# One block for both attentions, the top-1 stage and the experts, with the top-1 stage's first group computed inside the first attention

## The reference

```python
x = x + cross_attention(LN(x), ctx)     # 16 heads of 8, with biases
x = x + top1_ffn(LN(x))                 # 8 experts, one 128x128 matrix each
x = x + causal_attention(LN(x), ctx)    # keys and values again from ctx
x = x + top2_ffn(LN(x))                 # 8 experts, hidden width 352, SiLU gate

def top1_ffn(x):                        # x is LN(x) here
    chosen = argmax(x @ gate_w.T)       # 8 scores for each token
    return x + (x @ expert_w[chosen].T)
```

## Time and profile before

| what | value |
|---|---|
| median of 3 runs | 794.02 us (790.98 to 795.57) |
| the profiled execution | 793.19 us, its span 791.5 us |
| granted TensorE clock, mean | 0.907 of full speed |
| busy: PE, DVE, ACT, POOL | 78%, 61%, 50%, 45% |
| first attention, first to last instruction | 114.68 to 259.59 us of the span |
| first `choose` of the top-1 stage | 270.94 us |
| period from group to group in the top-1 stage | 14.05 us |

### The profile page before, as it was taken

How to read it: one execution, slowest core, us unless ns; L and a number is a source line. 1 busy time by engine, 2 the same in 40 slices (tenths; PEclk the granted TensorE clock), 3 DMA queues, 4 the chain that set the end, 5 groups by cost and what they waited for, 6 DMA issues and landing times.

```text
span 791.5 us, 22885 instructions
## 1 busy us (share of the span) xinstructions
PE 619.9 (78%) x8205; PEld 473.8 (60%) x8205; DVE 483.2 (61%) x1255; ACT 392.2 (50%) x901; POOL 359.4 (45%) x555
## 2 busy tenths in 40 slices
PE   1583548999999599999899888888740999999970
PEld 1352236777776354554566666666530999999970
DVE  1462257777773367667667988889534455555535
ACT  0684335777777224443367666666630444444430
POOL 5384351111010234445245577877874455555650
PEclk9697677999999699999799999999955999999995
DMA  3479850434400593577711543400011222222219
GB/s 75 123 249 177 189 193 3 109 95 111 96 4 2 108 268 143 188 277 247 295 49 40 102 106 106 103 26 26 26 44 54 55 66 70 59 63 67 63 34 318
DMA packets 65087, 87.58 MB, mean 111 GB/s; under 512 B 11209, under 2 KB 52433, under 8 KB 64977
## 3 DMA queue, kind: packets, MB, share of 16 engines
q1 hardware_dynamic: 56400, 75.04, 33.9%
q0 software_dynamic: 4352, 8.99, 3.6%
q10 hardware_dynamic: 4224, 2.10, 0.9%
HBM read 43.99 MB, written 41.96 MB: 109 GB/s over the span
## 4 chain that ended last, share of the span: by engine, by line
PE 36%; DVE 13%; issue 6%; POOL 5%; ACT 5%; DMA 2%; SPq 1%; ACTq 0%; POOLq 0%; DVEq 0%
PE bank L1567 12%; PE bank L1575 6%; PE bank L1410 5%; DVE nm L929 3%; POOL sorted_in L1130 2%; ACT pr L814 2%; POOL pr L1100 1%; DMA kk<-results 1%; DVE e0ch L1351 1%; PE bank L697 1%; PE bank L1555 1%; PE bank L753 1%; PE bank L1391 1%; PE bank L726 1%; PE bank L715 1%
## 5 line engine op out<-in xcount | busy, mean ns | idle before, releaser
L814 ACT ACTIVATE pr<-bank 128x512 f32<-128x512 f32 x256 | 146.9, 603 | 76.0 <-PE bank L700 73.4
L929 DVE TENSOR_REDUCE nm<-bank 128x8 f32<-128x1024 f32 x128 | 155.7, 1221 | 38.9 <-PE bank L674 37.7
L1567 PE MATMUL bank<-exxt,qq 128*128 128x128 f32 (+1 forms) x864 | 109.2, 277 | 0.7 <-ACT exxt L1605 0.7
L1567 PEld LDWEIGHTS bank<-exxt,qq 128*128 128x128 f32 (+1 forms) x864 | 101.3, 185 | 1.1 <-ACT exxt L1605 1.1
L1100 POOL TENSOR_SCALAR_AFFINE_SELECT pr<-pr 128x1024 f32<-128x1024 f32 x64 | 69.7, 1090 | 56.8 <-ACT pr L814 56.1
L1541 POOL DMA_INDIRECT results<-exy,exre x72 | 71.3, 990 | 29.8 <-issue 29.0
L715 PE MATMUL bank<-pr,values 128*9 128x128 f32 x2048 | 81.6, 278 | 2.4 <-POOL pr L1100 2.4
L697 PE MATMUL bank<-qq,kk 48*128 48x128 bf16 x1024 | 75.4, 221 | 3.4 <-ACT pr L814 2.4
L1410 PE MATMUL bank<-e0ch,expert_w 128*128 128x512 f32 x128 | 70.8, 635 | 6.4 <-DVE e0ch L1351 6.4
L700 PE MATMUL bank<-mt,pick 64*128 64x128 bf16 x1024 | 75.5, 221 | 0.0
L1642 DVE TENSOR_TENSOR exhi<-bank,exsi 128x384 f32<-128x384 f32 x72 | 40.1, 557 | 54.7 <-PE bank L1567 43.6
(11 more groups left out here) (209 smaller groups left out, 1160.9 us busy)
## 6 DMA issues: line engine op xcount, KB each, us to landing
sorted_in<-values SPq DMA_DIRECT2D x25, 715.0 KB, 5.7
k_parts<-pj_parts SPq DMA_DIRECT2D x16, 384.0 KB, 4.3
kk<-k_parts SPq DMA_DIRECT2D x64, 96.0 KB
qq<-q_parts SPq DMA_DIRECT2D x64, 96.0 KB
exx<-sorted_in SPq DMA_DIRECT2D x72, 65.0 KB
kk<-k_parts SPq DMA_DIRECT2D x64, 64.0 KB
qq<-q_parts SPq DMA_DIRECT2D x64, 64.0 KB
q_parts<-pj_parts SPq DMA_DIRECT2D x8, 384.0 KB, 4.1
```

Of the source, the lines that this page charges most:

```text
L814: act.activation(probs[c], st_bank[(n * NC + c) % ST][:], ACT.Exp, scale=scale).then_inc(exp_s, 1)
L929: dve.tensor_reduce(neg_max[n % 2][:, u * 2 * C4:(u + 1) * 2 * C4], score_banks(n, u).rearrange("q (h k) -> q h k", k=T), AX_X, ALU.max, n ...
L1567: mm = pe.matmul(to[q.p][0:fn, f * T:(f + 1) * T], own_w[q.p][:, w0 + f0:w0 + f0 + fn], x, start=True, stop=True)
```

## The change

Both attentions, the top-1 stage, the experts and `combine` now stand in one block; the `clear_semaphores()` between the first attention and the rest is gone. The first group's chain moves into the first attention's periods, at seven places that constants name: `stats` in period 24, `row_rstd` in 26, `apply` in 28, `turn` and `keep_turned` in 30, `score` in 31, `route` and the `spread` of experts 0 and 1 in 32. The attentions now share one set of tiles. Waits on the first attention's counters stand where PSUM banks are reused. SP issues the weights of the last step ahead of the causal keys, right behind the first attention's own loads, and each group of causal keys waits until the first attention has read the buffer it overwrites. The three small DVE operations that prepare the causal routing now stand ahead of the first attention, and POOL's second clearing of `max_parts` is gone.

```diff
+HEAD_STATS, HEAD_POWER, HEAD_APPLY, HEAD_TURN, HEAD_SCORE, HEAD_ROUTE, HEAD_SPREAD = B - 8, B - 6, B - 4, B - 2, B - 1, B, B
...
-        def attention(l, own, ahead_of_it=None):
+        def attention(l, own, tiles, follower=None, ahead_of_it=None):
...
                     if seq(n + AHEAD):
                         scores(n + AHEAD, 0)
+                    if not causal and n == HEAD_TURN:
+                        follower.turn(pe, FIRST)
...
+                    if not causal and n == HEAD_SCORE:
+                        follower.score(pe, FIRST)
+                    if not causal and n == HEAD_SPREAD:
+                        follower.spread(pe, FIRST, 0)
+                        follower.spread(pe, FIRST, 1)
                     if seq(n - 2):
                         project_out(n - 2)
...
                     if seq(n):
                         exponential(n, 1)
+                    if not causal and n == HEAD_APPLY:
+                        follower.apply(act, FIRST)
+                    if not causal and n == HEAD_TURN:
+                        follower.keep_turned(act, FIRST)
...
                     if seq(n + AHEAD):
                         reduce_pair(n + AHEAD, 0)
+                    if not causal and n == HEAD_STATS:
+                        follower.stats(dve, FIRST)
+                    if not causal and n == HEAD_ROUTE:
+                        follower.route(dve, FIRST)
...
                     if not causal and seq(n + 2):
                         split(n + 2)
+                    if not causal and n == HEAD_POWER:
+                        row_rstd(pool, FIRST, follower.ln)
...
+            def turn(pe, g):
+                if g.n == 0:
+                    pe.wait_ge(cross.max_s, B * (NC // 2))
                 pe.wait_ge(ln.xn_s, g.n + 1)
...
+            def spread(pe, g, e):
+
+                if g.n == 0 and e == 0:
+                    pe.wait_ge(cross.exp_s, B * NC)
...
-                for g in range(QK_BUFS):
+                load_weights()
+                for g in sorted(range(QK_BUFS), key=lambda g: (g - NG) % QK_BUFS):
+                    sp.wait_ge(cross.st_ps, (NG - QK_BUFS + (g - NG) % QK_BUFS + 1) * G * (NC // 2))
                     load_side(sp, 1, g, "k", early_in[1])
-                load_weights()
                 sp.wait_ge(tagged, 1)
...
-                row_rstd(pool, FIRST, ln)
                 add_rows(FIRST)
                 row_rstd(pool, FIRST.after(), ln)
                 add_rows(FIRST.after())
+                pool.wait_ge(cross.pv_s, B * NC)
...
-                stats(FIRST)
-                route(FIRST)
                 body(FIRST, first=True)
...
-                turn(FIRST)
-                score(FIRST)
                 body(FIRST, first=True)
...
-                apply(FIRST)
-                keep_turned(FIRST)
                 body(FIRST, first=True)
...
-        clear_semaphores()
...
             with nc.Block() as block:
                 @block.sync
                 def _(sp):
+                    cross.sync(sp)
                     top1.sync(sp)
...
                 def _(dve):
                     causal.clear_vector(dve)
+                    cross.vector(dve)
                     top1.vector(dve)
...
                 def _(pool):
-                    causal.clear_gpsimd(pool)
+                    cross.gpsimd(pool)
                     top1.gpsimd(pool)
```

More of the change, by code:

```diff
@@ L1266, in store_queries, with score @@
                 store_parts(sp, q_parts[g.n], parts[g.p], q_out[g.p])
+            def turn(pe, g):
+                if g.n == 0:
+                    pe.wait_ge(cross.max_s, B * (NC // 2))
+                pe.wait_ge(ln.xn_s, g.n + 1)
+                pe.wait_ge(kept, earlier(g.n))
+                for t in range(G):
+                    mm = pe.transpose(t_bank[:, t * T:(t + 1) * T], ln.xn[g.p][:, t, :], ident[:])
+                mm.then_inc(turned, 1)
+            def score(pe, g):
+                pe.wait_ge(kept, g.n + 1)
+                pe.wait_ge(tie_s, earlier(g.n))
+                for t in range(G):
+                    mm = pe.matmul(sc_bank[:, t * E:(t + 1) * E], xn_t[g.p][:, t * T:(t + 1) * T], gate0_w[:],
+                                   start=True, stop=True)
+                mm.then_inc(sc_ps, 1)
@@ new lines, in spread @@
+            def spread(pe, g, e):
+                if g.n == 0 and e == 0:
+                    pe.wait_ge(cross.exp_s, B * NC)
+                if e == 0:
+                    pe.wait_ge(hot_s, g.n + 1)
+                pe.wait_ge(chosen_s, earlier(g.n * E + e - 1))
+                for t in range(G):
+                    mm = pe.matmul(hot_bank[e % 2][:, t * T:(t + 1) * T],
+                                   hot[g.p][:, t, e:e + 1].broadcast_to([128, 128]), ident4[:, 0, :],
+                                   start=True, stop=True)
+                mm.then_inc(hot_ps, 1)
@@ new lines, in apply, with keep_turned, stats @@
+            def apply(act, g):
+                act.wait_ge(turned, earlier(g.n - 1))
+                act.wait_ge(sum_s, earlier(g.n - 1))
+                row_apply(act, g, x_of(g), ln)
+            def keep_turned(act, g):
+                act.wait_ge(turned, g.n + 1)
+                act.wait_ge(sc_ps, earlier(g.n - 1))
+                act.wait_ge(chosen_s, earlier((g.n - 1) * E))
+                act.copy(xn_t[g.p][:], t_bank[:]).then_inc(kept, 1)
+            def stats(dve, g):
+                row_stats(dve, g, x_of(g), ln)
@@ L1355, in body @@
                     if not last:
-                        stats(g.after())
+                        stats(dve, g.after())
                     choose(g, 1)
@@ L1367, in body @@
                     if not last:
-                        route(g.after())
+                        route(dve, g.after())
                     choose(g, 7)
@@ L1459, in body @@
                     if not last:
-                        apply(g.after())
-                        keep_turned(g.after())
+                        apply(act, g.after())
+                        keep_turned(act, g.after())
                     if not first:
@@ L1481, in experts0 @@
             stage.cut, stage.bias, stage.store_queries = cut, bias, store_queries
+            stage.turn, stage.score, stage.spread, stage.apply, stage.keep_turned = turn, score, spread, apply, keep_turned
+            stage.stats, stage.route, stage.ln = stats, route, ln
             stage.biased, stage.q_out, stage.q_ln, stage.rest0 = biased, q_out, q_ln, rest0
```

146 lines of the change are left out of this document (54 added, 92 removed).

## The result

The changed kernel takes 788.78 us (median of 8 executions, 786.74 to 790.41), the kernel before on the same chip 793.42 us (8 executions, 790.98 to 795.57). The ratio is 0.9944 with a 95% interval of 0.9925 to 0.9963: **faster by 4.64 us, 0.56%**. The profiled execution took 790.41 us and is the slowest of its eight, so what is read from it in microseconds compares with the 793.19 us of the execution profiled before.

What follows compares the result with a forecast made beforehand. The 11.35 us gap before the top-1 stage, with only the first group's chain running, was taken to set the end: 793.19 - 11.35 + 5.5 added work + 0.05 = 787.4 us, range 783.6 to 791.0.

Steps and rivals of the forecast that it cites:

- three conditions for being wrong: Attention ending over 7.2 us later, later top-1 groups lengthening, or causal attention starting less than 5 us earlier.
- Removed, 11.35 us: Between first attention's last sum and first `choose`: barrier, semaphore clearing and first group's chain go, saving 11.35 us.
- `stats`, 1.0: DVE statistics in period 24, between a reduction and `normalise`: adds 1.0 us, bounds 0 and 1.3.
- `apply`, 1.7: Four ACT activations in period 28, ahead of a copy TensorE needs: adds 1.7 us, bounds 1.5 and 1.8.
- `turn` and `keep_turned`, 1.0: Period 30, TensorE transposes and an ACT copy ahead of one TensorE awaits: adds 1.0 us, bounds 0.5 and 1.2.
- `score`, `route` and spreads, 1.8: Periods 31 and 32, ahead of a projection and a normalisation: together add 1.8 us, bounds 0.9 and 2.9.
- The moved loads, priced at 0: Six weight and 36 key loads moved to where DMA engines had little to do: cost 0.
- the tell it named: A longer period 22 would show that compute fails to cover the moved loads.
- The clock, priced at 0: At the seam, TensorE's clock falls again for as long as before and returns within the first group: 0 us.
- The first rival: TensorE's clock holds over the seam into the first experts, saving 1.4 us more: 786.0 us, 30% chance.
- Rival "the clock falls inside the attention": `apply`'s idle costs TensorE 2.4 GHz: short form +2.5, 790; long form, until top-1 stage, +7.6, 795; 14% chance.
- Rival "given back": Something with its own clock sets the top-1 stage's end, so the earlier start gains nothing: 793 us, 6% chance.

Runs made afterwards that it cites:

- e4: Changed kernel with the first group's chain back behind the attention in the one block, all loads last; 789.99 us, 0.9976 of the kernel before.
- e5: Changed kernel with all loads last, `route` moved behind `normalise` and the two spreads behind the projection; 782.73 us, 0.9873 of the kernel before.
- e6: Changed kernel with all loads last, `stats` and `apply` cut into single instructions, one per period, `row_rstd` in 25; 784.78 us, 0.9890 of the kernel before.
- e7: Changed kernel with the edits of e5 and e6, plus `turn` and `keep_turned` moved within period 30; 780.13 us, 0.9850 of the kernel before.
- e2: Changed kernel with causal key loads and weight loads both behind the first attention; 785.83 us, 0.9917 of the kernel before.
- e1: Changed kernel with the six weight loads issued behind the causal key loads, keys still inside the attention; 786.02 us, 0.9936 of the kernel before.
- e8: The changed kernel measured again with no edit; 787.57 us, 0.9931 of the kernel before.
- e3: Changed kernel with the weight loads still inside the first attention but the key loads behind it; 786.41 us, 0.9932 of the kernel before.
- e9: e7 with weight and key loads back inside the first attention, where the change put them; 783.61 us, 0.9895 of the kernel before.
- e10: Changed kernel with each group of key loads waiting one group of sequences longer, weights unmoved; 786.08 us, 0.9920 of the kernel before.

## Why the prediction was right, and where it was not

The forecast was 787.4 us, with 783.6 to 791.0 as its range; measured were 788.78, and faster by more than 0.5%, to which it gave 0.81. The gain forecast was 6.6 us against the median, and 4.64 were measured. That it came so near is in part luck. The sum was made for the profiled execution, and the one profiled now took 790.41, 3.0 us over it: the stall (2.95), the later start (1.11) and what was lost behind the top-1 stage (0.6) stood in no term, while the clock that held over the seam (1.24) and steps that cost 0.46 less than priced hid a part of them. The median lies 1.4 us over 787.4, because the profiled execution is the slowest of its eight. Two of its three conditions for being wrong were met: the attention ends 9.1 us later, over the 7.2, and the causal attention starts 3.5 us earlier instead of 5. The later groups did not lengthen.

- **Removed, 11.35 us:** right. The distance went to -0.09. e4 splits it in 1.1 for barrier and clearing and 10.2 for the chain.
- **`stats`, 1.0:** measured 0.88. **`row_rstd`, 0:** no step shows anything. **`apply`, 1.7:** 1.40; TensorE's idle was 1.36, where the twin in the causal attention had 1.52. So it lies under the bounds, 1.5 to 1.8: the step grew by no more than TensorE's idle, not by the whole 1.65 us of ACT's time. **`turn` and `keep_turned`, 1.0:** 1.08. **`score`, `route` and spreads, 1.8:** 0.89 + 0.79 = 1.68. Sum 5.04 against 5.5; each term but `apply` within its bounds. e5, e6 and e7 show that the causes were those named: moved off the place where TensorE waits, `stats`, `apply`, `route` and the pair in 30 cost nothing, but for the 0.18 us in e6. `score` was not moved in any run.
- **The moved loads, priced at 0:** this is the step that failed, by 2.95 us. The prediction read that periods with loads in flight ran no slower, and that the queue was free. It asked whether the data collides, but the same DMA engines also carry TensorE's own instruction fetch, which has no row among those that it read. Behind the weights' loads packet 20 started 6.2 us after record 5057 instead of 0.6 in the kernel before, and TensorE ran out of instructions. Even the tell it named was the wrong one: step 22 is long by `stats` alone, as in e2 without any load; the cost came in step 24.
- **The clock, priced at 0:** it held over the seam in the profiled execution, which gave 1.24 us. The first rival had 1.4 for it and 30%. The windows of the changed kernel over the seam:

```profile
264.00:266.00 2.00, 1.17 (x14) 1.16 (x15) 0.70 (x4) 0.85 (x2) 0.00 (x0) 1.00 0.41 92
266.00:268.00 2.00, 0.77 (x5) 0.39 (x5) 0.75 (x3) 0.27 (x1) 0.00 (x0) 1.00 0.26 76
268.00:270.00 2.00, 1.02 (x4) 0.56 (x5) 1.60 (x6) 0.00 (x0) 0.00 (x0) 1.00 0.00 0
```

  and of e1_weights_last over its own, which ends 3.1 us earlier:

```profile
262.00:264.00 2.00, 1.12 (x13) 0.79 (x10) 0.75 (x3) 0.00 (x0) 0.00 (x0) 0.96 0.25 66
264.00:266.00 2.00, 0.94 (x3) 0.50 (x2) 0.67 (x2) 0.27 (x1) 0.00 (x0) 0.50 0.58 103
266.00:268.00 2.00, 1.72 (x2) 0.66 (x3) 1.95 (x11) 0.00 (x0) 0.50 (x3) 0.50 1.05 375
```

  Nearly the same drain and the same busy times, and in e1 the clock falls to 0.50 at about 264. The first group, from `choose` to its last `choose`, took 10.7 us in three profiled executions (the change, e8, e7) and 11.5 to 13.1 in seven (e1, e2, e3, e5, e6, e9, e10). So "it falls" is the commoner case among them, as forecast, and this execution had the other. What decides isn't settled: one execution of each kernel has been seen, and kernels with the same drain differ.

  The rule of the Trainium skill that the prediction weighed ("TensorE: Matmul & The Clock Gate", section "Why this matters for your kernels") asks only for no long idle gap between bursts. By it the clock would have held in all of these, where TensorE's longest idle in the drain is 0.98 us; in seven of ten it did not.
- **Rival "the clock falls inside the attention":** its short form is real. In the change the fall came right behind the stall, at 236.4 us, ten microseconds ahead of `apply`. In e2, e3 and e5, which have no such stall, and in e8, which has one, the clock fell after `apply`. The timeline and the windows of e2_all_last:

```profile
245.38 0.66 PE L731 MATMUL bank<-ident,ot 128*128 128x128 f32 x4 [1.36 <-ACT ot L831]
```

```profile
244.00:246.00 2.00, 0.64 (x7) 0.63 (x6) 0.56 (x1) 2.00 (x7) 1.30 (x3) 1.00 0.00 0
246.00:248.00 2.00, 2.00 (x35) 1.28 (x33) 0.75 (x3) 0.48 (x1) 0.35 (x1) 0.53 0.04 8
```

  It costs 1.04 us in step 27 of e2 (4.87 instead of 3.83), 1.5 us in steps 26 and 27 of e8, under the 2.5 that the rival had, since the clock is back within a step. In the change, e1 and e10 the same idle left the clock at full speed. The long form was never seen.
- **Rival "given back":** 0.6 us of 3.5 at the start of the causal attention are missing at the end of the span. In 407 to 411 us the changed kernel has the clock at 0.5 to 0.6, and the kernel before has 1.00 there; this is no property of the change that an experiment showed.
- **Not in the prediction:** the first sum 1.11 us later. Over the kernels of the study, whose code is the same up to there, it came at 132.45 to 136.32 us. So it is within the spread of the stages ahead; the median of the eight executions lies 1.6 us under the profiled one.

## What to carry to other kernels

Work that fills a gap between stages is paid for in the steady periods that it is put into. Put it in pieces no longer than the wait that the engine has there anyway, and behind, not ahead of, what the busiest engine waits for next: the same instructions cost 5.0 us where the change put them and 0.9 in e7. When loads are moved under compute, look at the instruction-fetch queue in the DMA view too: bytes that nobody waits for can delay the instructions of the engine that everybody waits for. Here three placements of the loads had no stall (both kinds behind the attention, only one kind inside, keys one group later). The placements with the weights' loads inside came near it: in e10 a packet ended 1.29 us before its first instruction was due, in e3 1.45, against 2.2 and more in every kernel without the weights' loads inside.

## What was unexpected of the hardware

- TensorE's instructions come over the same 16 DMA engines as data, one 16 KB packet for each 256 records, fetched only one packet ahead. The next 256 instructions ran 1.46 us after the packet's end at the earliest in the four idles (1.28 us over all twelve traces). With no loads beside it packet 20 came 0.6 to 2.2 us after TensorE passed record 5057, with one kind 3.1 to 3.5, and at 5.4 to 6.3 us TensorE stood idle for 1.7 us, in all three executions. In two of them (the change, e9) the granted clock then fell to 0.5, and both together cost about 3 us; in e8 it stayed at 1.00.
- The granted clock fell in some executions and not in others after stretches with nearly the same instructions and busy times: over the seam in seven of ten, after `apply` in e2, e3, e5 and e8 and not in the change, e1 and e10; behind the fetch stall in two of three.
- Semaphore clearing and barrier between two blocks cost 1.1 us of the seam, one tenth of the gap.
